# Reading a table of numbers ahead of a loop on TensorE, and routing the first half of the tokens in two steps, in a ViT layer with a two-of-eight mixture of experts

## The chip, the cores and the metric

The kernel runs on one core of one Trainium2 chip. The number that counts is the device time of one execution in microseconds (us). The kernel before took 144.37 us as the median of three runs (144.24 to 144.65). The profiled execution took 144.59 us, of which the trace spans 142.8.

TensorE (PE) multiplies, VectorE (DVE), ScalarE (ACT) and GpSimd (POOL) work on tiles in SBUF and PSUM, SyncE (SP) issues transfers. Each engine takes its instructions in the order in which the program writes them, and waits on semaphores where the program says so.

## The reference

Sixteen images of 128 by 128 are cut in 64 patches each. One layer is computed, all of it in float32:

```python
g       = noisy_linear(patches, W1);  inner = noisy_linear(patches, W2)
h       = (g * tanh(softplus(g)) * inner) @ W3.T + b3 + position     # 16 x 64 x 128
h       = concat(cls_tok, h)                                          # one class row per image
n       = layernorm(h)
q, k, v = split(n @ w_qkv)                                            # 8 heads of 16
dots    = where(causal, q @ k.T * scale, 0)
t       = dots - cum_mean(dots);  s = cum_mean(t * t)                 # no softmax: a running norm
attn    = where(causal, t * rsqrt(s + eps) * norm_g + norm_b, 0)
h       = h + (attn @ v) @ w_out + b_out
x       = layernorm(h)
logits  = x @ router_w;  top 2 of 8 experts, gates = softmax of the two
y_e     = layernorm(x + relu(x @ w1[e] + b1[e]) @ w2[e] + b2[e]) * gamma[e] + beta[e]
out     = h + sum over the two experts of gate * y_e
```

The class row is the same for all images, so it is computed once and the layer works on 1025 rows.

## The kernel before

**Tiles.** The 1024 patch rows are 8 tiles of 128, with the class row as a ninth tile (number 4) between the two halves. Attention goes by four groups of four images (two tiles each). For each group PE makes scores into PSUM banks 0 to 3, DVE masks them into `D` (`evict`), ACT squares them, PE multiplies with the values (`weigh`) and sums the squares (`sum_squares`), DVE forms means and scales (`head_sums`, `mix`), PE projects (`turn_mixed`, `output`), and DVE adds the residual and normalises (`residual_sums`, `normalise_group`). The part of the sum that comes from the class key is the table `tab`. In the kernel before, PE adds it into the bank of the projection with a product of the identity and `tab` at the end of `sum_values` (line 1257).

**Routing.** The tokens are routed in three parts: the first half with the class row (tiles 0 to 4), then two tiles, then two tiles. For a part, PE turns the normalised rows (`turn_norm2`), ACT copies them out of PSUM (`copy_norm2`), PE multiplies with the router (`route`), DVE picks the top two (`choose`) and forms 0/1 tables (`rank_tables`), PE counts ranks with them (`rank_bases`, `rank`), and DVE makes row numbers of them (`places`). The gates of the first part are computed on POOL (lines 471 to 479), the others on DVE (`gates`) from an exponential on ACT. POOL then scatters each row twice to DRAM with indirect DMAs, 16 in all (`dispatch`, line 464): eight for the first half, four for each later part.

**The loop over slots.** The rows stand in DRAM sorted by expert, and 23 tiles of 128 rows (slots) are run through an expert each. The first five slots have a fixed expert; for the other 18 DVE computes the expert and the tile number (`slot_tiles`; its last step is line 1002, semaphore `slots_done`). Each engine that needs these numbers reads them from SBUF into registers, four with one load (`four_values`, line 323 in the profile). SP needs them for the transfers, ACT for the first seven, PE for the address of the second weight. PE reads four at a time inside the loop, at slots 5, 9, 13, 17 and 21. Per slot PE turns the rows (1430), multiplies with the first weight (1438) and one slot later with the second (1457); ACT applies relu (684), DVE normalises (1054 to 1076), and POOL adds the bias (498) and sends the rows back to DRAM (503). The last four slots are not sent: PE adds them with products of 0/1 matrices (1482).

**Filler.** `keep_warm(n, bank)` is n products of zeros that nobody reads (line 1150). Ten of them (`REWARM`) stand ahead of the loop, behind a wait for `token_cols_set`, which POOL sets after its last scatter (line 490). PE's order around the loop is this:

```python
pe.wait_ge(token_cols_set, 1)
keep_warm(REWARM, 7)
pe.wait_ge(slots_done, 2)
pe.wait_ge(w2_loaded, 16)
pe.wait_ge(base_done, 3)
turn_slots(0)
```

All orders are written out by hand; there is no scheduler.

Of the kernel before, what the change touches and what calls it, by code (L numbers as in the profile page):

```python
# [10 lines left out]
ALU = mybir.AluOpType  # L11
# [30 lines left out]
PART_AT, PART_T = [0, CLS + 1, CLS + 1 + CT // 2], [CT, CT // 2, CT // 2]  # L42
PATCH_TILE = [0, CT, CT + CT // 2]
# [35 lines left out]
def vit_tower(nc, patches, noise, body, b1, w1b1, w2, gb2, out):  # L79
    ctx = ExitStack()  # L80
    with ctx:  # L81
# [49 lines left out]
        minus_one = sb("minus_one", [P, NT])  # L131
# [78 lines left out]
        WARM, KEEP_WARM, REWARM = 16, [11, 12, 2, 2, 5, 3, 1, 2, 1, 3, 2], 10  # L210
        TABLES = 9 + PARTS
        X2_BANK, LG_BANK, RANK_BANK, COUNT_BANK, GATE_BANK = [6, 0, 4], [7, 1, 5], [2, 3, 6], 0, 7
# [70 lines left out]
        first_gates = sem("first_gates")  # L283
# [59 lines left out]
        def _(sp):  # L343
# [29 lines left out]
            sp.wait_ge(first_gates, 4)  # L373
# [27 lines left out]
            for j in range(FIXED, FIRST_ROWS):  # L401
                load_pack(j)
# [20 lines left out]
        def _(pool):  # L423
            nc.gpsimd.memset(e_base[:, :], math.e).then_inc(pow_const, 1)
            nc.gpsimd.memset(minus_one[:, :], -1.0).then_inc(pow_const, 1)
# [27 lines left out]
            pool.wait_ge(pow_const, 2)  # L453


            def dispatch(t, c):
                pool.wait_ge(row_at_done, c + 1)
                if c == 0:
                    pool.wait_ge(first_gates, 4)
# [16 lines left out]
            pool.wait_ge(first_gates, 2)  # L476
            nc.gpsimd.tensor_tensor(x2k[:, a:b, 0, P + 1], den[:, a:b], minus_one[:, a:b], ALU.pow).then_inc(first_gates, 1)
            pool.wait_ge(first_gates, 3)
# [38 lines left out]
        def _(act):  # L517
# [92 lines left out]
            def copy_norm2(c):  # L610

                a = PATCH_TILE[c] * P
                act.wait_ge(x2T_ps, c + 2)
                nc.scalar.copy(x2T[:, a:a + PART_T[c] * P], ps[:, X2_BANK[c], 0:PART_T[c] * P]).then_inc(x2T_done, 1)
# [32 lines left out]
            nc.scalar.copy(x2T_cls[:, :], ps[:, LG_BANK[0], BANK - 1:BANK]).then_inc(x2T_cls_done, 1)  # L647
            square(2)
            copy_norm2(0)
# [7 lines left out]
            copy_norm2(1)  # L657
# [50 lines left out]
        def _(dve):  # L708
# [207 lines left out]
            def residual_sums(g):  # L916
                at = GROUP_AT[g]
                dve.wait_ge(proj_ps, g + 2)
                nc.vector.tensor_tensor(acc[:, at:at + GT, :], ps[:, 6 + g % 2, GT * P:2 * GT * P].rearrange("p (t d) -> p t d", d=P),
# [7 lines left out]
            def choose(c):  # L927
                a, b = ROUTED[c]
                n = b - a
                dve.wait_ge(logits_ps, c + 1)  # L930
                dve.wait_ge(tables_set, TABLES)
                for t in range(a, b):
                    nc.vector.max(top[:, t, :], ps[:, LG_BANK[c], (t - a) * SW:(t - a) * SW + EXPERTS]).then_inc(topped, 1)
                dve.wait_ge(topped, b)
                nc.vector.tensor_tensor(dlt[:, a:b], top[:, a:b, 1], top[:, a:b, 0], ALU.subtract).then_inc(dlt_done, 1)  # L935
                for t in range(a, b):
                    nc.vector.max_index(top_at[:, t, :], top[:, t, :], ps[:, LG_BANK[c], (t - a) * SW:(t - a) * SW + EXPERTS]).then_inc(top_index, 1)
# [88 lines left out]
            choose(1)  # L1026
            normalise_group(3)
# [3 lines left out]
            choose(2)  # L1031
# [4 lines left out]
            dve.wait_ge(first_gates, 4)  # L1036
# [85 lines left out]
        def _(pe):  # L1122
# [60 lines left out]
            def cls_column():  # L1183
# [3 lines left out]
                nc.tensor.transpose(ps[:, LG_BANK[0], BANK - 1:BANK], x2[0:1, CLS, :], ident[0:1, 0:1]).then_inc(x2T_ps, 1)  # L1187
# [48 lines left out]
            def sum_values(g):  # L1236
# [11 lines left out]
                if g == 2:  # L1248
                    pe.wait_ge(x2T_done, 1)
                if g == 3:  # L1250
                    pe.wait_ge(top_index, ROUTED[0][1])
                for i in range(GI):
                    n = GI * g + i
                    mm(ps[PATCHES * (i % 2):PATCHES * (i % 2 + 1), 6 + g % 2, i // 2 * P:(i // 2 + 1) * P], after[:, :],
                       vb[:, n, :, 0:2 * HD], start=True, stop=True)
                pe.wait_ge(tab_set, 1)
                mm(ps[:, 6 + g % 2, GT * P:2 * GT * P], ident, tab[:, :].unsqueeze(1).to_broadcast([P, GT, P]),
                   start=True, stop=False).then_inc(vsum_ps, 1)

            def weigh(g, lo=0, hi=GI):  # L1260
# [5 lines left out]
                if g >= 2:  # L1266
                    pe.wait_ge(oT_done, g - 1)
                for i in range(lo, hi):
# [25 lines left out]
            def output(g):  # L1294

                pe.wait_ge(oT_done, g + 1)
                for t in range(GT):
                    last = mm(ps[:, 6 + g % 2, (GT + t) * P:(GT + t + 1) * P], oT[:, (g * GT + t) * P:(g * GT + t + 1) * P], bd("wout"),
                              start=False, stop=(t == GT - 1))
                last.then_inc(proj_ps, 1)  # L1300

            def turn_norm2(c):

                if c == 0:
                    pe.wait_ge(acc_done, 2)
                else:
                    pe.wait_ge(D_done, GROUPS)
                for i in range(PART_T[c]):
                    t = PART_AT[c] + i
                    pe.wait_ge(x2_done, PATCH_TILE[c] + i + 2)  # L1310
                    last = nc.tensor.transpose(ps[:, X2_BANK[c], i * P:(i + 1) * P], x2[:, t, :], ident)
# [258 lines left out]
```

## Time and profile before

| | |
|---|---|
| median of 3 runs | 144.37 us (144.24 to 144.65) |
| profiled execution | 144.59 us, span 142.8 us |
| PE busy | 130.9 us, 92% of the span |
| DVE / ACT / POOL busy | 104.4 / 72.9 / 57.3 us |
| start of the loop over slots (first product, line 1438) | 84.83 us |
| end of the loop (first product of line 1482) | 129.73 us |

The page's first table counts an engine as busy while an instruction runs. PE is busy 92% of the span, but some of that is filler and some of it runs at half clock. So the chain of waits and the timelines say more than the shares.

### The profile page before, as it was taken

How to read it: one execution, taken by the hardware profiler on the slowest of the kernel's cores; microseconds unless marked ns; L12 is line 12 of the kernel's file. 1: busy time of each engine (PE TensorE's matmuls, PEld its weight loads, DVE VectorE, ACT ScalarE, POOL GpSimd, SP SyncE). 2: the span in 40 equal slices, each digit the busy share in tenths (PEclk: the TensorE clock that was granted, in tenths of full speed). 3: DMA queues.
4: the chain of work that ended last, by engine and by line, in shares of the span. 5: the costliest groups of instructions: out<-in, count | busy, mean ns of one | idle time of the engine just before them, and what ended most of it. 6: DMA issues, size and time to landing. Idle time of an engine off the chain costs nothing. (4 is left out here: it accounts for less than half of the span.)

```text
span 142.8 us, 3886 instructions
## 1 busy us (share of the span) xinstructions
PE 130.9 (92%) x1210; PEld 114.2 (80%) x1210; DVE 104.4 (73%) x417; ACT 72.9 (51%) x214; POOL 57.3 (40%) x96
## 2 busy tenths in 40 slices
PE   7999899999999999889993899999999999999960
PEld 7944898788759898668930879999999999999950
DVE  1479999979988667778664029887878789988580
ACT  5534315834476531139900006887878977896000
POOL 8900000000000046775778131377677767680010
PEclk9999999999999999999555569999999999999999
DMA  4999399999993019611115477598999751015405
GB/s 117 263 457 418 156 387 414 404 339 274 278 270 113 5 17 333 255 50 56 45 56 101 179 166 221 133 317 277 243 334 311 239 163 41 21 33 167 175 0 149
DMA packets 16423, 28.47 MB, mean 199 GB/s; under 512 B 1793, under 2 KB 9878, under 8 KB 16276
## 3 DMA queue, kind: packets, MB, share of 16 engines
q1 hardware_dynamic: 13700, 25.43, 55.3%
q0 software_dynamic: 1152, 2.07, 4.3%
q10 hardware_dynamic: 1552, 0.73, 2.2%
q8 instruction: 10, 0.16, 0.5%
q14 instruction: 9, 0.07, 0.1%
HBM read 19.55 MB, written 12.09 MB: 222 GB/s over the span
## 5 line engine op out<-in xcount | busy, mean ns | idle before, releaser
L1457 PE MATMUL ps<-w_all,hid 128*128 (+1 forms) x184 | 24.7, 278 | 0.3 <-issue 0.2
L1457 PEld LDWEIGHTS ps<-w_all,hid 128*128 128x128 f32 x184 | 22.4, 192 | 1.0 <-issue 0.8
L503 POOL DMA_INDIRECT back<-kTm,xg x16 | 15.9, 997 | 12.2 <-ACT kTm L693 6.1
L684 ACT ACTIVATE hid<-ps,D 128x128 f32<-128x128 f32 x48 | 13.5, 362 | 13.7 <-PE ps L1438 13.7
L1150 PE MATMUL ps<-zeros 128*128 128x128 f32 x112 | 17.8, 312 | 2.9 <-POOL SQ L490 2.9
L1150 PEld LDWEIGHTS ps<-zeros 128*128 128x128 f32 x112 | 16.1, 222 | 3.9 <-POOL SQ L490 3.4
L471 POOL TENSOR_TENSOR ex<-e_base,dlt 128x5 f32<-128x5 f32 x1 | 1.2, 1207 | 44.8 <-DVE dlt L935 44.8
L464 POOL DMA_INDIRECT rows<-x2k,row_at x16 | 16.1, 1007 | 6.9 <-issue 5.0
L1054 DVE COPY xgT<-ps 128x128 f32<-128x128 f32 x23 | 6.7, 290 | 10.1 <-PE ps L1430 8.4
L1438 PE MATMUL ps<-xgT,D 128*128 128x128 f32 x96 | 12.8, 276 | 0.0
L684 ACT ACTIVATE hid<-ps,last_parts 128x128 f32<-128x128 f32 x44 | 12.4, 364 | 0.0
L1438 PEld LDWEIGHTS ps<-xgT,D 128*128 128x128 f32 x96 | 11.7, 192 | 0.1
L1438 PE MATMUL ps<-xgT,last_parts 128*128 128x128 f32 x88 | 11.6, 275 | 0.0
L689 ACT ACTIVATE ysd<-ymv,moe_eps 128x1 f32<-128x1 f32 x23 | 6.8, 294 | 8.4 <-DVE ymv L1063 8.4
L1438 PEld LDWEIGHTS ps<-xgT,last_parts 128*128 128x128 f32 x88 | 10.7, 192 | 0.0
L498 POOL TENSOR_TENSOR xgb<-xg,D 128x128 f32<-128x128 f32 x12 | 6.1, 509 | 5.4 <-issue 4.8
L1061 DVE BATCH_NORM_STATS2 yst<-y 128x6 f32<-128x128 f32 x23 | 6.8, 294 | 0.8
L1131 PE MATMUL ps<-xT_oT,w_noisy 128*128 128x512 f32 x16 | 7.2, 603 | 0.0
L1138 PE MATMUL ps<-zeros 128*128 128x128 f32 x32 | 6.2, 383 | 1.1 <-DVE ln_eps L713 1.1
L1138 PEld LDWEIGHTS ps<-zeros 128*128 128x128 f32 x32 | 6.0, 295 | 1.1 <-DVE ln_eps L713 1.1
L1430 PE MATMUL ps<-body_sb,xg 128*128 128x128 f32 x23 | 6.5, 283 | 0.3 <-DMA xg<-rows 0.2
L693 ACT ACTIVATE kTm<-u,yg 128x128 f32<-128x128 f32 x16 | 6.6, 412 | 0.0
(236 smaller groups left out, 278.4 us busy)
## 6 DMA issues: line engine op xcount, KB each, us to landing
rows<-blank SPq DMA_DIRECT2D x8, 589.5 KB, 6.7
D<-pack SPq DMA_DIRECT2D x12, 386.0 KB, 5.2
last_parts<-pack SPq DMA_DIRECT2D x11, 386.0 KB, 4.8
pack<-w1b SPq DMA_DIRECT2D x1, 2064.0 KB, 15.6
w_all<-w SPq DMA_DIRECT2D x1, 2048.0 KB, 12.2
back<-zeros SPq DMA_DIRECT2D x1, 1152.0 KB, 9.0
xg<-rows SPq DMA_DIRECT2D x16, 65.5 KB, 3.0
xT_oT<-patches SPq DMA_DIRECT2D x2, 512.0 KB, 5.9
```

Source lines behind the costliest of these rows:

```text
L464: nc.gpsimd.indirect_dma_start(rows, bass.IndirectOffsetOnAxis(ap=row_at[:, k, t:t + 1], axis=0), x2k[:, t, k, :], None, bounds_check=EXPE ...
L503: nc.gpsimd.indirect_dma_start(back, bass.IndirectOffsetOnAxis(ap=xg[j][:, P:P + 1].bitcast(U32), axis=0), z[j], None, bounds_check=P * K ...
L684: nc.scalar.activation(hid[j % 2][:, f, :], ps[:, 2 + 2 * (j % 2) + f // 2, f % 2 * P:(f % 2 + 1) * P], ACT.Relu, bias=packed[j % NW][:, H ...
L689: nc.scalar.activation(ysd[j % 2][:, :], ymv[j % 2][:, 1:2], ACT.Sqrt, bias=moe_eps[:, 0:1]).then_inc(y_sd, 1)
L693: nc.scalar.activation(z[j], u[j % 2][:, :], ACT.Copy, scale=yg[j % 2][:, 0:1]).then_inc(z_done, 1)
L1054: nc.vector.tensor_copy(xgT[j % 2][:, :], ps[:, j % 2, 0:P]).then_inc(xgT_done, 1)
L1061: nc.vector.bn_stats(yst[j % 2][:, :], y[j % 2][:, :]).then_inc(y_stats, 1)
L1131: last = mm(ps[:, IN_BANK[c][k], :], w_noisy[:, 2 * k + half, :], xT[:, c, half, :], start=(half == 0), stop=(half == HALVES - 1))
L1138: mm(ps[:, 6, 0:P], zeros[:, :], zeros[:, :], start=True, stop=True)
L1150: mm(ps[:, bank, 0:P], zeros[:, :], zeros[:, :], start=True, stop=True)
L1438: last = mm(ps[:, 2 + 2 * (j % 2) + f // 2, f % 2 * P:(f % 2 + 1) * P], packed[j % NW][:, f * P:(f + 1) * P], xgT[j % 2][:, :], start=True ...
L1457: last = mm(ps[:, 6 + j % 2, 0:P], hid[j % 2][:, f, :], w2_all[:, bass.ds(expert_j, 1), f, :].rearrange("p a n -> p (a n)"), start=(f == 0 ...
```

## The change

The change has these parts.

- **PE's numbers.** PE waits for `slots_done` and reads all 18 expert numbers ahead of the filler and the loop, with five loads in a row. Inside the loop it reads none.
- **SP's order.** SP issues the packs of slots 5 and 6 after the rows of the last four slots, not before.
- **The class key's table.** POOL adds `tab` to `h` for each half (two instructions of 128x512). PE's product with the identity goes, and `residual_sums` waits for the new semaphore `h_tab`.
- **The first half's logits.** The first half is turned and routed group by group: group 0 and the class row ahead of `scores(3)`, group 1 between the two halves of `weigh(2)`. `choose` is called once for tiles 0 and 1 and once for tiles 2 to 4. `sum_values(2)` moves ahead of `scores(3)`, `sum_values(3)` to the place that it leaves. The five fillers ahead of `scores(3)` are gone; two more stand behind `output(2)`. Banks of the logits are other ones, and `output(2)` waits until they have been read.
- **First gates.** The reciprocal goes from POOL (a power of -1) to DVE.
- **The later parts.** DVE normalises the last group after the row numbers of the second part, not ahead of its tables. PE turns the last two tiles after `rank(1)`. ACT computes the second part's exponential ahead of the copy `twice(1)`.

```diff
-        WARM, KEEP_WARM, REWARM = 16, [11, 12, 2, 2, 5, 3, 1, 2, 1, 3, 2], 10
+        WARM, KEEP_WARM, REWARM = 16, [11, 12, 2, 2, 0, 5, 1, 2, 1, 3, 2], 10
...
+            pool.wait_ge(tab_set, 1)
+            for c in range(CHUNKS):
+                pool.wait_ge(xn_done, LN_TILES[c + 1][1] if c else 1 + CT)
+                some = h[:, CHUNK_AT[c]:CHUNK_AT[c] + CT, :]
+                nc.gpsimd.tensor_tensor(some, some, tab[:, :].unsqueeze(1).to_broadcast([P, CT, P]), ALU.add).then_inc(h_tab, 1)
...
-            nc.gpsimd.tensor_tensor(x2k[:, a:b, 0, P + 1], den[:, a:b], minus_one[:, a:b], ALU.pow).then_inc(first_gates, 1)
...
-            for j in range(FIXED, FIRST_ROWS):
-                load_pack(j)
+            expert_at(0)
             tile_at(FIRST_ROWS - FIXED)
             for j in range(SENT, SLOTS):
                 tile_at(j - FIXED)
             for j in range(SENT, SLOTS):
                 load_rows(sp, j, tile_at(j - FIXED))
+            for j in range(FIXED, FIRST_ROWS):
+                load_pack(j)
... ACT
-            twice(1)
             nc.scalar.activation(table_scrap[:, 3:4], zeros[:, 0:1], ACT.Exp)
             exp_gates(1)
-            copy_norm2(2)
+            twice(1)
+            copy_norm2(3)
... DVE
             normalise_group(1)
+            choose(0, GT, 1)
             evict(3)
-            choose(0)
+            choose(GT, CLS + 1, 2, 0)
             rank_tables(0)
             head_sums(2)
+            dve.wait_ge(first_gates, 2)
+            nc.vector.reciprocal(x2k[:, 0:CLS + 1, 0, P + 1], den[:, 0:CLS + 1]).then_inc(first_recip, 1)
             places(0)
...
-            choose(1)
-            normalise_group(3)
+            choose(*ROUTED[1], 3, 1)
             rank_tables(1)
             gates(1)
             places(1)
-            choose(2)
+            normalise_group(3)
+            choose(*ROUTED[2], 4, 2)
... PE, sum_values
-                pe.wait_ge(tab_set, 1)
-                mm(ps[:, 6 + g % 2, GT * P:2 * GT * P], ident, tab[:, :].unsqueeze(1).to_broadcast([P, GT, P]),
-                   start=True, stop=False).then_inc(vsum_ps, 1)
+                last.then_inc(vsum_ps, 1)
... PE
             cls_column()
-            keep_warm(KEEP_WARM[4], 6)
+            turn_norm2(0)
+            sum_values(2)
+            route(0)
             scores(3)
-            turn_norm2(0)
+            turn_norm2(1)
             weigh(2, 0, GI // 2)
-            route(0)
+            route(1)
             weigh(2, GI // 2, GI)
             sum_squares(2)
             rank_bases(0)
             rank(0)
-            sum_values(2)
+            sum_values(3)
             weigh(3)
...
-            w2_experts = {}
+            pe.wait_ge(slots_done, 2)
+            w2_experts = list(range(FIXED))
+            for s in range(0, FREE, 4):
+                w2_experts += list(four_values(mybir.EngineType.PE, expert_of, s, EXPERTS - 1))
...
             pe.wait_ge(token_cols_set, 1)
             keep_warm(REWARM, 7)
-            pe.wait_ge(slots_done, 2)
             pe.wait_ge(w2_loaded, 16)
```

How the orders stand is shown at three places. The first is PE ahead of the loop and in it. In a row of order, L is the line, and ISA is a register instruction. Before, from the product with the gates (1422, 1424), with the reading of slots 5 to 8 at the end:

```order
L1422 MATMUL ps<-beta_sel,gateT 128x512 x2
L1424 MATMUL ps<-beta_sel,gateT 1x128
L1150 MATMUL ps<-zeros 128x128 x10
L1430 MATMUL ps<-body_sb,xg 128x128 x2
...
L1438 MATMUL ps<-xgT,D 128x128 x4
L323 TENSOR_LOAD expert_of
L323 ISA x8
L1457 ISA
L1457 MATMUL ps<-w_all,hid 128x128
```

The same place in the changed kernel, where the pair of a load and its eight register instructions stands four times, and then once with four:

```order
L1441 MATMUL ps<-beta_sel,gateT 128x512 x2
L1443 MATMUL ps<-beta_sel,gateT 1x128
L321 TENSOR_LOAD expert_of
L321 ISA x8
...
L321 ISA x4
L1162 MATMUL ps<-zeros 128x128 x10
L1449 MATMUL ps<-body_sb,xg 128x128 x2
...
L1457 MATMUL ps<-xgT,D 128x128 x4
L1473 ISA
L1473 MATMUL ps<-w_all,hid 128x128
```

Five loads and 36 register instructions have moved from the loop to a place behind the wait for `slots_done` and ahead of the ten fillers.

The second place is PE between `scores(2)` and `weigh(3)`. Before (1187 the class column, 1311 turns, 1321 to 1324 the router, 1254 and 1257 `sum_values`):

```order
L1187 MATMUL ps<-body_sb,x2k 128x1
L1150 MATMUL ps<-zeros 128x128 x5
L1232 MATMUL ps<-qT,kTm 128x64 x16
L1311 MATMUL ps<-body_sb,x2k 128x128 x4
L1272 MATMUL ps<-vb,D 64x34 x8
L1321 MATMUL ps<-body_sb,last_parts 128x28 x4
L1323 MATMUL ps<-body_sb,zeros 128x28
L1324 MATMUL ps<-body_sb,x2T_cls 1x28
...
L1254 MATMUL ps<-vb,after 64x128 x4
L1257 MATMUL ps<-tab,body_sb 128x256
L1272 MATMUL ps<-vb,D 64x34 x16
```

In the changed kernel (1325 turns, 1337 to 1342 the router, 1264 `sum_values`, 1244 the scores):

```order
L1199 MATMUL ps<-body_sb,x2k 128x1
L1325 MATMUL ps<-body_sb,x2k 128x128 x2
L1264 MATMUL ps<-vb,after 64x128 x4
L1337 MATMUL ps<-body_sb,last_parts 128x28 x2
L1341 MATMUL ps<-body_sb,zeros 128x28
L1342 MATMUL ps<-body_sb,x2T_cls 1x28
L1244 MATMUL ps<-qT,kTm 128x64 x16
L1325 MATMUL ps<-body_sb,x2k 128x128 x2
L1282 MATMUL ps<-vb,D 64x34 x8
L1337 MATMUL ps<-body_sb,last_parts 128x28 x2
...
L1264 MATMUL ps<-vb,after 64x128 x4
```

Half of the turns, half of the router's products and the class row now stand ahead of the scores, and the product with `tab` is gone.

The third place is DVE from the choice of the second part. Before (933 to 937 `choose`, 766 and 769 `normalise_group(3)`, 943 to 950 the tables, 957 to 961 the gates, 967 and 972 the row numbers):

```order
L937 MAX_INDEX top_at<-top,ps 128x8 x2
L766 RECIPROCAL rstd<-ln_dev 128x2
L769 TENSOR_SCALAR x2k<-acc,mv,rstd 128x128 x2
L943 TENSOR_TENSOR hot<-iota,top_at 128x2x16
...
L967 TENSOR_TENSOR hot_place<-hot,ps 128x2x16
L972 TENSOR_REDUCE row_at<-hot_place 128x2x2
L933 MAX top<-ps 128x8 x2
```

In the changed kernel:

```order
L946 MAX_INDEX top_at<-top,ps 128x8 x2
L952 TENSOR_TENSOR hot<-iota,top_at 128x2x16
...
L976 TENSOR_TENSOR hot_place<-hot,ps 128x2x16
L981 TENSOR_REDUCE row_at<-hot_place 128x2x2
L769 RECIPROCAL rstd<-ln_dev 128x2
L772 TENSOR_SCALAR x2k<-acc,mv,rstd 128x128 x2
L940 MAX top<-ps 128x8 x2
```

The normalising of the last group has moved behind the row numbers of the second part.

## Rows read from the trace of the kernel before

**Rows 1.** The page, span in 40 slices: PE's granted clock, in tenths.

```profile
PEclk9999999999999999999555569999999999999999
```

**Rows 2.** Chain that ended last, 77 to 96 us: start, duration, what.

```profile
77.05 4.59 DMA rows<-x2k,row_at
...
87.89 0.11 PE ps L1430
...
95.47 0.11 PE ps L1430
```

**Rows 3.** PE's timeline, 72 to 127 us: start, duration, instructions (f32 products show as two).

```profile
72.03 3.78 PE L1422 MATMUL ps<-beta_sel,gateT 72*128 72x512 f32 x4 [0.35 <-ACT gateT L671]
...
79.20 4.64 PE L1150 MATMUL ps<-zeros 128*128 128x128 f32 x20 [2.88 <-POOL SQ L490]
84.00 0.90 PE L1430 MATMUL ps<-body_sb,xg 128*128 128x128 f32 x2 [0.16 <-DMA xg<-rows]
84.83 1.16 PE L1438 MATMUL ps<-xgT,D 128*128 128x128 f32 x8
...
85.94 1.06 PE L1438 MATMUL ps<-xgT,last_parts 128*128 128x128 f32 x8
...
95.42 1.06 PE L1438 MATMUL ps<-xgT,D 128*128 128x128 f32 x8
...
126.87 1.06 PE L1438 MATMUL ps<-xgT,D 128*128 128x128 f32 x8
```

**Rows 4.** DVE's timeline, end of the slot numbers.

```profile
73.62 0.18 DVE L1002 TENSOR_SCALAR tile_of<-tile_f 128x18 int32<-128x18 f32 x1
```

**Rows 5.** Line 323 on ACT, whole span: ns min/median/max, first and last start.

```profile
L323 ACTq TENSOR_LOAD <-tile_of x1: 508/508/508, 73.8 to 73.8; - x1
```

**Rows 6.** Line 323, window 94 to 97 us.

```profile
L323 PEldq SEQ_ASSERT  x4: 18/18/28, 95.4 to 96.4; - x4
L323 PEldq TENSOR_LOAD <-expert_of x1: 556/556/556, 94.5 to 94.5; - x1
```

**Rows 7.** Line 323, window 102 to 105 us.

```profile
L323 PEldq FUSED_REGOPS  x4: 146/148/151, 103.1 to 103.9; - x4
...
L323 PEldq TENSOR_LOAD <-expert_of x1: 340/340/340, 102.7 to 102.7; - x1
```

**Rows 8.** PE's timeline, 45 to 58 us.

```profile
45.63 1.38 PE L1150 MATMUL ps<-zeros 128*128 128x128 f32 x10
47.14 1.12 PE L1232 MATMUL ps<-qT,kTm 32*128 32x64 f32 x32
48.19 0.66 PE L1311 MATMUL ps<-body_sb,x2k 128*128 128x128 f32 x4
...
49.62 1.07 PE L1321 MATMUL ps<-body_sb,last_parts 128*128 128x28 f32 x8
50.54 0.39 PE L1323 MATMUL ps<-body_sb,zeros 128*128 128x28 f32 x2
...
54.29 0.70 PE L1257 MATMUL ps<-tab,body_sb 128*128 128x256 f32 x2
```

**Rows 9.** DVE's timeline, 65 to 68 us.

```profile
65.28 0.60 DVE L769 TENSOR_SCALAR x2k<-acc,mv,rstd 128x128 f32<-128x128 f32 x2
...
67.12 0.19 DVE L972 TENSOR_REDUCE row_at<-hot_place 128x4 uint32<-128x32 f32 x1
```

**Rows 10.** ACT's timeline, the load of the exponential's table.

```profile
64.67 1.28 ACT L660 ACT_TABLE_LOAD   x1
```

**Rows 11.** POOL's timeline, 68 to 85 us and 123 us.

```profile
68.11 0.97 POOL L464 DMA_INDIRECT rows<-x2k,row_at  x1 [1.57 <-DVE row_at L972]
...
84.00 0.45 POOL L498 TENSOR_TENSOR xgb<-xg,D 128x128 f32<-128x128 f32 x1 [4.85 <-issue]
...
123.25 0.99 POOL L503 DMA_INDIRECT back<-gT,xg  x1 [0.91 <-ACT gT L693]
```

More of the change, by code:

```diff
@@ L646, in _ @@
             act.wait_ge(x2T_ps, 1)
-            nc.scalar.copy(x2T_cls[:, :], ps[:, LG_BANK[0], BANK - 1:BANK]).then_inc(x2T_cls_done, 1)
+            nc.scalar.copy(x2T_cls[:, :], ps[:, CLS_COL_BANK, BANK - 1:BANK]).then_inc(x2T_cls_done, 1)
+            copy_norm2(0)
             square(2)
-            copy_norm2(0)
+            copy_norm2(1)
             square(3)
@@ L1296, in output @@
                 pe.wait_ge(oT_done, g + 1)
+                if g == 2:
+                    pe.wait_ge(top_index, ROUTED[0][1])
                 for t in range(GT):
                     last = mm(ps[:, 6 + g % 2, (GT + t) * P:(GT + t + 1) * P], oT[:, (g * GT + t) * P:(g * GT + t + 1) * P], bd("wout"),
-                              start=False, stop=(t == GT - 1))
+                              start=True, stop=True)
                 last.then_inc(proj_ps, 1)
@@ L1304, in turn_norm2 @@
                 if c == 0:
-                    pe.wait_ge(acc_done, 2)
-                else:
+                    pe.wait_ge(v_done, 2 * GROUPS)
+                if c == 1:
+                    pe.wait_ge(x2T_done, 1)
+                if c == 2:
                     pe.wait_ge(D_done, GROUPS)
[L1308 to L1311, printed above, removed]
+                for i in range(GT):
+                    pe.wait_ge(x2_done, GT * c + i + 2)
+                    at = X2_AT[c] + i * P
+                    last = nc.tensor.transpose(ps[:, X2_BANK[c], at:at + P], x2[:, GROUP_AT[c] + i, :], ident)
                 last.then_inc(x2T_ps, 1)
@@ L1316, in route @@
                 pe.wait_ge(x2T_done, c + 1)
-                pe.wait_ge(x2T_cls_done, 1)
+                if c == 1:
+                    pe.wait_ge(top_index, GT)
+                part = max(c - 1, 0)
                 router_wide = body_sb[:, BODY_AT["router"][0]:BODY_AT["router"][0] + SW]
-                for i in range(PART_T[c]):
-                    at = (PATCH_TILE[c] + i) * P
-                    last = mm(ps[:, LG_BANK[c], i * SW:(i + 1) * SW], x2T[:, at:at + P], router_wide, start=True, stop=True)
+                for i in range(GT):
+                    at = LG_AT[part] + (GROUP_AT[c] - ROUTED[part][0] + i) * SW
+                    last = mm(ps[:, LG_BANK[part], at:at + SW], x2T[:, (c * GT + i) * P:(c * GT + i + 1) * P], router_wide, start=True, stop=True)
                 if c == 0:
-                    mm(ps[:, LG_BANK[c], CLS * SW:(CLS + 1) * SW], zeros[:, :], router_wide, start=True, stop=True)
-                    last = mm(ps[0:1, LG_BANK[c], CLS * SW:(CLS + 1) * SW], x2T_cls[:, :], router_wide, start=True, stop=True)
+                    pe.wait_ge(x2T_cls_done, 1)
+                    at = LG_AT[0] + CLS * SW
+                    mm(ps[:, LG_BANK[0], at:at + SW], zeros[:, :], router_wide, start=True, stop=True)
+                    last = mm(ps[0:1, LG_BANK[0], at:at + SW], x2T_cls[:, :], router_wide, start=True, stop=True)
                 last.then_inc(logits_ps, 1)
@@ L1392, in _ @@
             turn_mixed(2)
-            sum_values(3)
             output(2)
```

73 lines of the change are left out of this document (34 added, 39 removed).

## The prediction

> **What bounds the kernel now.** I read the chain that ended last first. It ends in the loop over slots, where PE's products follow one another without a gap, and it goes back from there over the loading of the first rows and the landing of the last scatter (81.64) to POOL's run of scatters [rows 2]. So two things set the time: when the loop starts, and how long PE takes in it. Then I read PE's timeline ahead of the loop [rows 3]: PE waits for POOL until 79.20, runs ten fillers (20 passes) at half clock until 83.84, and finds the rows of slot 0 at 84.00. The filler ends only 0.16 us before the data: two chains of nearly the same length meet here. The page's slices show the granted clock at half (1.2 GHz) from slice 20 to 23 and in part of slice 24, which ends at 85.7, and at full (2.4 GHz) elsewhere [rows 1]. In the last step I read line 323, the reading of numbers, since the change moves it into just this stretch [rows 5 to 7].
>
> **The scatters' side.** PE is busy without a gap from 47.14 to the end of `sum_squares(3)`, so what leaves this stretch shortens it [rows 8]. Two of four turns: half of the 0.59 from 48.19 to the next instruction, 0.3. Two of four router products: half of 49.62 to 50.54, 0.46. The zero product and the class row: 0.45, by the nearest row (0.39 for the zero product, overlapped, and one shorter). The product with `tab`: 0.63 of its 0.70. Sum 1.8 us. The work that moves ahead of `scores(3)` (0.3 turns, 0.55 `sum_values(2)`, 0.9 router) takes the place of 1.38 us of filler and 0.1 of waiting, so `scores(3)` starts within 0.3 us of 47.14. DVE's first `choose` lies in its wait for the scores. The two additions on POOL stand where POOL does nothing; by its 128x128 addition of 0.45 us [rows 11] each costs between 0.45 and 1.8, I take 1.6, and nobody waits for them, as the residual that needs them is some 9 us away. The reciprocal moved to DVE (0.2) takes a power off POOL and brings the first scatter forward, but POOL waits for the second part's row numbers anyway (1.57 idle ahead of 68.11 [rows 11]).
>
> The second part's row numbers came at 67.31 [rows 9]. They come 1.8 earlier by PE, and 0.7 earlier since the normalising steps behind them (0.60 and its reciprocal). Of the 0.7 a part is lost to the exponential: the table load of 1.28 us on ACT [rows 10] starts only 0.4 earlier by the moved copy, and the gates wait 0.2 to 0.3 for what follows it. Row numbers at 65.1, so 2.2 earlier. The last eight scatters, the landing of 4.59 us and the rows of slot 0 follow: slot 0's rows would be there at 81.8, and `token_cols_set` at 76.9. Taking the packs of slots 5 and 6 out of this stretch can only shorten the landing; they are wanted ten us later and cost nothing.
>
> **The numbers' side.** What this side needs is `slots_done`, 73.80 [rows 4]. It comes from the last group, and there the gain is given back: the normalising that used to stand at 65.28 now stands behind `places(1)`, which ends at 65.1, so it starts at 65.3 again. Everything behind it (turn, copy, router, ranks, counts, on a PE at half clock) is as before. I take `slots_done` at 73.8, with 0.5 us either way for errors of the sums above.
>
> PE's sequencer can start to read then: the trace shows it reading at 94.5 while products issued before run until 96.48 [rows 3, 6], so the products with the gates (72.03 to 75.8 and one more [rows 3]) do not hold it up. ACT began its own reading at 73.8 [rows 5]. A group of four took PE 1.9 us the first time (94.5 to 96.4), 1.5 us the next (102.7 to 104.2), with 0.27 per number: a register operation of 0.15 and what follows it [rows 5 to 7]. All five in a row: 1.7 for the first with a load of about 0.5, three of 1.45, and 1.0 for the last with two numbers, 7.0 us in all. The bounds are 4.7 (18 numbers at 0.165, the two register instructions of each without what lies between them, and five loads at 0.34) and 8.7 (four groups at the first one's 1.9 and 1.1 for the last); I keep to the pace of rows 7, as nothing but the place is different. So the filler starts at 80.8, not at the 76.9 that POOL would allow. Ten fillers keep the array for 4.4 us at half clock: PE is free at 85.2. Slot 0 starts there, against 84.00, and the products at 86.05 against 84.83: 1.2 later. I add 0.1, since the clock came back shortly before the first product, and would now come back in it. If it returns while the filler runs, the filler is shorter and the delay is 0.6 to 0.8.
>
> The Trainium skill, page "DMA: Bandwidth & Descriptors", section "Latency and other measured facts", gives a floor of about 600 ns for a `tensor_load` and calls unrolling by four the way to spread it. By that figure alone an estimate would be 5 x 0.6 = 3.0 us, numbers at 76.8, and no delay of the filler at all. The rows show a shorter load (0.34 to 0.56) but as much again and more in the register operations behind it, which the page does not count.
>
> **In the loop.** A slot takes (95.47 - 87.89) / 4 = 1.895 us where no numbers are read [rows 2]. From slot 1's product (85.94) to slot 22's (126.87, both [rows 3]) there are 21 steps, 39.7 us at that pace (the last has no turn, 0.11), and it took 40.9: 1.2 us are lost at the reads, 0.47 of them at the first, about 0.2 to 0.3 at each of the next three. All of it comes back to PE. Of the end, DVE's last additions wait for the rows sent back, and the send at 123.25 waited for slot 16's result [rows 11], which lies behind the first three reads only. So I count 0.9 to 1.2, and take 0.95. What could swallow it is DVE, whose work per slot adds up to about 1.8 us, close to PE's 1.895; 0.2 of loss there is in the range.
>
> **The sum.** Against the profiled execution: +1.25 at the start, -0.95 in the loop, +0.3 in all, so 144.9 against 144.59. The median of the runs is 0.2 lower, so I forecast 144.6. The gain of 2.2 us on the scatters is hidden behind PE's numbers and filler. Its own range is 144.0 to 145.2. A difference of 0.3% (0.43 us) is about what a measurement of this kernel can tell from none.
>
> **Rivals.**
> - *The filler shrinks.* The numbers take 6 us or less, and the clock returns within the filler, as it would if it came at the time of before (84.6) regardless of PE's start. PE free at 84.6, products 0.6 later or less, loop -1.1: -0.5 to -0.9, 143.6. For it: passes take 0.11 at full clock and 0.22 at half. Against: before, the clock came back only after all of the filler was done. Chance 0.22.
> - *The numbers cost only their loads.* Then the full 2.2 us come through, and 0.95 in the loop: 144.4 - 3.15 = 141.2. For it: between 103.1 and 104.2 half of the time is not spent in a register operation. Against it: even without those gaps the reading ends at 78.5 [rows 7], behind POOL's 76.9. Chance 0.05. The floor per load on the Trainium skill's page on DMA leads to this case.
> - *The clock returns late.* PE now stands idle from 76.3 to 80.8, not to 79.2, at half clock. If the clock comes back one slice of the page (3.57 us) later than 86.2, all products until then run at half pace: 1.8 us more, in all +2.0, 146.4; half a slice gives 145.5. The same mechanism acts earlier too: less work on PE after 58 us may let the clock fall before the last group is routed (it fell near 67.5), which moves `slots_done` by 0.5. It decides from about 1 us of half clock inside the loop on. For it: the stretch has long gaps already; against: the filler is as long as before and ends right at the loop. Chance 0.20.
> - *The change on the first half fails*, that is, PE does not gain the 1.8 us, as DVE's `choose` or POOL's gates hold up `rank(0)`. Then `slots_done` moves as well, by what is missing, up to 1.5 us: 145.2 to 146. Chance 0.05.
>
> **Chances and range.** The forecast has 0.48, of which 0.06 lies above the band of no change and 0.04 below. Faster by over 0.3%: 0.04, 0.18 of the 0.22 of the first rival, and 0.05, 0.27 in all. Slower by over 0.3%: 0.06 + 0.20 + 0.05 = 0.31, to which I move 0.03 from the band for a start of the numbers held up by something that the trace does not show. Within: 0.38 + 0.04 - 0.03 = 0.39. The range that leaves out 2 in 10 is 143.4 to 146.0.
>
> **What the changed profile would show.** PE's reading (five loads, no product between them) from about 73.8 to 80.8; PE's idle time ahead of the filler ended by nothing on POOL, whose last instruction ahead of it (line 490 before) ends near 77; first slot at 85.2 with its rows landed some 3 us before; the last scatter issued near 74.9, not 77.05; all steps of the loop 1.89 us. A loop that starts before 83, or a filler that waits for POOL again, would make the forecast wrong, and so would a clock row with a sixth slice at half.

## The result and the profile after

The changed kernel took 146.03 us (median, 145.87 to 146.42) against 144.48 us for the kernel before on the same chip: a ratio of 1.0113, 95% interval 1.0086 to 1.0139. It is 1.55 us slower, where no change was forecast (144.6) and the range ended at 146.0.

The page's clock row and the landmarks of PE and DVE answer to [rows 1], [rows 3] and [rows 4]. First the granted clock in 40 slices of the changed kernel's span of 144.0 us:

```profile
PEclk9999999999999999997555558999999999999997
```

It has five slices at half clock with a part of one on either side, against four and a part before [rows 1].

PE's timeline of the changed kernel (start, duration, instructions). Line 1441 is the product with the gates, 1162 the filler, 1449 the turn of a slot's rows, 1457 the first product:

```profile
72.47 3.78 PE L1441 MATMUL ps<-beta_sel,gateT 72*128 72x512 f32 x4 [0.35 <-ACT gateT L674]
...
82.17 4.63 PE L1162 MATMUL ps<-zeros 128*128 128x128 f32 x20 [5.40 <-issue]
86.60 0.64 PE L1449 MATMUL ps<-body_sb,xg 128*128 128x128 f32 x2
87.40 1.16 PE L1457 MATMUL ps<-xgT,D 128*128 128x128 f32 x8 [0.17 <-DVE xgT L1066]
...
131.18 2.17 PE L1497 MATMUL ps<-gT,xT_oT 128*128 128x128 f32 x18
```

The filler used to start at 79.20, after 2.88 us of waiting for POOL. It starts at 82.17 now, after 5.40 us of "issue", which is time in which the profile shows no other engine that it waits for. What PE's sequencer (the part of the engine that takes the instructions and reads the registers) does in it stands in line 321, window 73 to 83 us (duration in ns, first and last start), beside the last step of the slot numbers on DVE and two POOL instructions. The first stands behind the last scatter, and the second is the first use of slot 0's rows, so that they have arrived by then:

```profile
L321 PEldq FUSED_REGOPS  x18: 146/146/165, 75.1 to 81.9; - x18
L321 PEldq SEQ_ASSERT  x18: 18/18/24, 75.3 to 82.1; - x18
L321 PEldq TENSOR_LOAD <-expert_of x5: 331/347/590, 74.4 to 81.0; - x5
```

```profile
74.16 0.18 DVE L1011 TENSOR_SCALAR tile_of<-tile_f 128x18 int32<-128x18 f32 x1
```

```profile
76.63 1.14 POOL L492 IOTA SQ<- 128x1152 f32 x1
80.91 0.45 POOL L500 TENSOR_TENSOR xgb<-xg,D 128x128 f32<-128x128 f32 x1 [3.15 <-issue]
```

Three chains stand side by side. Scatters: POOL's last instruction starts at 76.63, not 78.03, and slot 0's rows are there by 80.91, not at 84.00 [rows 3, 11]. That is 3.1 us of gain, but PE touches these rows only at 86.60. Numbers: they are ready for reading at 74.34, not at 73.80, and read by 82.1. Filler: 4.4 us behind that. The first product comes 2.57 us later than before (87.40 against 84.83), and from there to the last stage 43.78 us pass instead of 44.90, 1.12 less. The sum is +1.45 us. The medians differ by 1.55 us, and the two profiled executions (145.87 and 144.59) by 1.28: the last stage and what follows it took 0.17 less in the changed one.

### The profile page after: what moved, and what is told of

It is laid out like the page before. It is cut to its first block and busy times, and to the rows that moved or that the text cites. A ratio compares the mean times of both kernels' runs of the same rounds, so it can differ in the third digit from the quotient of the medians.

```text
span 144.0 us, 3863 instructions
## 1 busy us (share of the span) xinstructions
PE 126.7 (88%) x1196; PEld 112.1 (78%) x1196; DVE 104.3 (72%) x418; ACT 73.0 (51%) x215; POOL 58.1 (40%) x96
## 5 line engine op out<-in xcount | busy, mean ns | idle before, releaser
L1162 PE MATMUL ps<-zeros 128*128 128x128 f32 x106 | 16.9, 314 | 5.4 <-issue 5.4
L1162 PEld LDWEIGHTS ps<-zeros 128*128 128x128 f32 x106 | 15.3, 224 | 6.4 <-issue 6.4
L470 POOL TENSOR_TENSOR h<-h,tab 128x512 f32<-128x512 f32 x2 | 2.5, 1266 | 28.5 <-DVE tab L909 23.7
L1150 PE MATMUL ps<-zeros 128*128 128x128 f32 x32 | 5.9, 370 | 1.1 <-DVE ln_eps L716 1.1
L1071 DVE TENSOR_TENSOR y<-ps,xgb 128x128 f32<-128x128 f32 x23 | 6.5, 282 | 0.1
L1150 PEld LDWEIGHTS ps<-zeros 128*128 128x128 f32 x32 | 5.7, 282 | 1.1 <-DVE ln_eps L716 1.1
```

The source lines that it names most:

```text
L1150: mm(ps[:, 6, 0:P], zeros[:, :], zeros[:, :], start=True, stop=True)
L1162: mm(ps[:, bank, 0:P], zeros[:, :], zeros[:, :], start=True, stop=True)
```

## The experiments

Three landmarks serve in every run: the end of the slot numbers on DVE (line 1002 or 1011), the first product of the loop, and the first product of the last stage. The two stretches between them can be compared even where the time of a whole run can't. Runs e1 to e4 and f1 to f4 fell on two chips on which the kernel before took 150 to 156 us (medians 152.39 and 153.83), and whose traces hold a long wait between 56 and 67 us of the span (last section). For those the stretches and the ratio to the kernel before on the same chip are used; the intervals are wide, and no trace of the kernel before was kept from these chips. Runs g1 to g4 and h1 to h4 fell on two other chips, on which the medians of the kernel before were 144.56 and 144.41 us.

Two theories run through the expectations. Theory 1: the reading of the 18 numbers and then the filler, one behind the other, set the start of the loop. Theory 2: this reading costs nothing, and another part of the change costs the time.

| run | numbers to first product | first product to last stage | ratio to before (95%) |
|---|---|---|---|
| before (profile) | 11.03 | 44.90 | |
| changed (profile) | 13.06 | 43.78 | 1.0113 (1.0086 to 1.0139) |
| e1 reads in the loop | 8.72 | 44.82 | too few runs |
| f1 the same | 8.72 | 44.93 | too few runs |
| h1 the same | 8.71 | 44.82 | 0.9894 (0.9839 to 0.9948) |
| e2 before, reads ahead | 13.20 | 44.22 | 1.0121 (1.0008 to 1.0234) |
| f2 the same | 12.59 | 43.82 | 1.0113 (1.0061 to 1.0164) |
| e3 reads between fillers | 8.74 | 43.77 | 0.9932 (0.9868 to 0.9996) |
| e4 more filler at rank(1) | 12.86 | 43.95 | 1.0188 (1.0076 to 1.0300) |
| g4 the same | 12.72 | 43.80 | 1.0133 (1.0064 to 1.0202) |
| g1 changed, again | 12.61 | 43.78 | 1.0135 (1.0081 to 1.0188) |
| g2 no filler | 8.82 | 46.13 | 0.9938 (0.9904 to 0.9973) |
| g3 filler first | 12.56 | 46.14 | 1.0221 (1.0151 to 1.0290) |
| f3 reads in loop, packs back | 9.14 | 45.12 | 0.9816 (0.9732 to 0.9901) |
| h2 the same | 8.90 | 45.02 | 0.9924 (0.9897 to 0.9951) |
| f4 four groups, more filler | 7.34 | 45.20 | 0.9681 (0.9583 to 0.9779) |
| h4 the same | 7.38 | 43.80 | 0.9732 (0.9690 to 0.9773) |

**The reads undone (e1, f1, h1).** The changed kernel with `four_values` back in `second_product` (shortened; the function again reads four numbers when it meets a slot that has none yet):

```diff
-            pe.wait_ge(slots_done, 2)
-            w2_experts = list(range(FIXED))
-            for s in range(0, FREE, 4):
-                w2_experts += list(four_values(mybir.EngineType.PE, expert_of, s, EXPERTS - 1))
+            w2_experts = {}            # four numbers are read at slots 5, 9, 13, 17, 21
...
             keep_warm(REWARM, 7)
+            pe.wait_ge(slots_done, 2)
```

> The changed kernel, but PE reads the expert numbers four at a time inside the loop again and waits for slots_done behind the filler; all else as changed. Theory 1 (reading 18 numbers and then the filler, in series, set the start of the loop): the filler starts with POOL's last instruction near 77.9 and ends near 82.3, the first product of the loop starts near 83.0 instead of 87.4, and the loop loses about 1.1 us at the reads again: 146.0 - 4.4 + 1.1 = 142.7 us. Theory 2 (the first half's new order or SP's new order costs the time): the time stays at 146 us or above, since the loss in the loop comes on top.

> The same kernel as e1 (the changed kernel with PE's reads inside the loop again), beside others on one chip. From slot numbers (end of the last step of slot_tiles) to the first product of the loop both theories can be read in the trace: theory 1 expects 8.7 us as in e1 against 13.1 in the changed kernel, and 1.1 us more inside the loop, so 3.3 us off the changed kernel and 1.8 off the kernel before. Theory 2 (the first half's order costs) expects it no faster than the kernel before.

> The kernel of e1 and f1 (reads in the loop, all else as changed), once more. On a chip where the kernel before takes 144.5 us, theory 1 expects 142.2 to 142.9 us (8.7 us from the slot numbers near 74.5 to the first product, 1.1 us lost in the loop); the theory that the rest of the change costs time as well expects 144 us or more.

Measured: 143.27 us in h1 against 144.41 (ratio 0.9894). The interval lies below the kernel before and, beside g1's 1.0135, below the changed kernel. On the other chips the medians were 149.84 against 152.39 (e1) and 150.70 against 153.83 (f1), of four runs each. The stretch from numbers to first product is 8.71 us in all three, and the 1.1 us in the loop are back. PE's timeline of h1:

```profile
78.28 4.64 PE L1162 MATMUL ps<-zeros 128*128 128x128 f32 x20 [1.05 <-POOL SQ L492]
82.72 0.60 PE L1449 MATMUL ps<-body_sb,xg 128*128 128x128 f32 x2
83.52 1.16 PE L1457 MATMUL ps<-xgT,D 128*128 128x128 f32 x8 [0.20 <-DVE xgT L1066]
```

The filler waits for POOL again, and slot 0's rows, in use on POOL at 80.60, now wait for the filler: 2.1 us. So theory 1 holds, and the rest of the change is a gain by itself. My figure for h1 (142.2 to 142.9) was 0.4 to 1.1 us too good. Its first product came at 83.52 and not near 83.0, since POOL's last instruction ran at 77.09 and not at 76.63 as in the changed kernel's trace; what the rest is, the traces don't tell.

**The reads alone (e2, f2).** The kernel before with the reverse edit.

> The kernel before, and of the change only PE's reading ahead of the filler and the loop. Theory 1: the numbers are there at 73.8 + 7.7 = 81.5, the filler ends near 85.9, the first product starts near 86.7 instead of 84.83, and the loop gains 1.1: 144.5 + 1.9 - 1.1 = 145.3 us. Theory 2: the reads cost nothing at this place and the loop gains, 143.4 us.

> The same kernel as e2 (the kernel before with the reads ahead of the filler alone). Theory 1: 13.2 us from slot numbers to first product against 11.0 before, 1.1 us back in the loop: 1.0 us slower than the kernel before, ratio 1.007. Theory 2: 0.8% faster than before.

Measured: ratios 1.0121 and 1.0113, both intervals above 1. By the ratios, the edit that moves five reads costs as much on the old order as the whole change does. The two stretches show less of it: against the kernel before, e2's add up to 1.5 us more and f2's to 0.5, of some 1.7 by the ratios. Nothing on record shows where the rest lies. In e2 the clock came back only within the first product (1.61 us long, 1.16 in f2), which accounts for the 0.4 by which its loop took longer than f2's.

**Reads between the fillers (e3).** Two fillers stand ahead of each of the five reads, and PE doesn't wait for POOL any more (shortened):

```diff
-            pe.wait_ge(slots_done, 2)
-            w2_experts = list(range(FIXED))
-            for s in range(0, FREE, 4):
-                w2_experts += list(four_values(...))
+            pe.wait_ge(slots_done, 2)
+            for s in range(0, FREE, 4):
+                keep_warm(2, 7)
+                read_experts(s)
...
-            pe.wait_ge(token_cols_set, 1)
-            keep_warm(REWARM, 7)
```

> The changed kernel, with the ten fillers spread over the five reads (two ahead of each) and without the wait for POOL's last instruction. Theory 1: only the reading (7.7 us from 74.4) is left in series, the rows of slot 0 are there at 80.9, so the first product starts near 83.0: 4.4 us earlier, 141.6 us with a clock that returns as early relative to the loop as before. Rival on the clock: fillers with pauses of over a microsecond between them do not bring the clock back, the first products run at half pace until it returns, and up to 1.8 us of it are lost: 143.4 us. Theory 2: 146 us.

Measured: first product 8.74 us after the numbers, not 13.06, with the loop as short as in the changed kernel (43.77). The clock was at full by the first product (1.16 us for its eight passes), so in this execution the rival on the clock did not occur; it did once in h3, below. The time was a miss: a ratio of 0.9932 is 143.5 us where the kernel before takes 144.5, and not 141.6. The interval allows 142.6 to 144.4, and the runs don't tell where the rest of the gain went.

**More filler behind `rank(1)` (e4, g4).** One line, `keep_warm(4, 2)`, ahead of `turn_norm2(3)`.

> The changed kernel with four more fillers behind rank(1), where PE stood idle for 1.1 us ahead of turning the last two tiles. If the early fall of the clock (near 65 instead of 67.5) came from this idle stretch, the clock stays up as before, slots_done comes 0.5 us earlier than 74.35 and the whole is 0.5 us faster: 145.5 us. If the fall does not hang on this stretch, nothing changes: 146.0 us, or 0.1 to 0.3 more by fillers in the way of the turn.

> The same kernel as e4 (the changed kernel with four more fillers behind rank(1)), beside the changed kernel on the same chip. If the earlier fall of the clock comes from PE's idle stretch there, the clock stays at full through the ranks of the last part, the slot numbers come 0.5 to 1.1 us earlier, and the whole is 0.5 to 1.1 us faster than g1. Rival: the clock falls anyway, no difference.

Inconclusive. The trace of g4 has the clock at full through 66 to 68 us and the numbers at 73.50, 1.2 us earlier than g1's 74.71, but the medians are the same (145.95 and 146.01), with g4's runs from 144.9 to 146.9. In the same window the granted clock was 0.50 in g1 and 0.72 in the changed kernel's first trace, so two executions of one kernel already differ. One profiled execution with more filler and a late fall of the clock does not show that the filler caused it.

**No filler (g2), filler first (g3), and the changed kernel beside them (g1).** g2 sets `REWARM` to 0. g3 moves the wait for `token_cols_set` and the ten fillers ahead of the wait for `slots_done` and the reads.

> The changed kernel itself, beside the next three on one chip. Both theories: 1.1% slower than the kernel before; from slot numbers to first product 13.1 us.

> The changed kernel with no filler ahead of the loop (REWARM 0). Theory 1 (reads and filler in series): the first product comes 4.5 us earlier, 8.6 us after the slot numbers, but at half clock. If the clock comes back as long after PE's start as it did with the filler (5.2 us), the first slots lose 2.6 us: 1.9 us less than the changed kernel in all. Rival (the filler is what brings the loop up to pace and is worth its time): as slow as the changed kernel or slower.

> The changed kernel with the filler ahead of the wait for slots_done and of the reads, behind POOL's last instruction. If PE's sequencer runs ahead of the array, the reads begin about 1 us after the filler starts (near 79 instead of 74.4) and end near 86.7: the first product 13 us after the slot numbers, as in the changed kernel, within 0.7 us. The array then idles 4 us between filler and loop, so the clock can fall back or stay down and the first slots lose up to 2.6 us: 0 to 2.6 us slower than the changed kernel. If the sequencer waited for the array, the first product comes 3.5 us later still.

g2 took 143.89 us, 2.1 less than g1, 1.9 expected. The first product comes 3.8 us sooner after the numbers and the loop takes 2.35 longer, as it starts at half clock. That is 1.4 us; of the rest, the numbers came 0.2 earlier in g2's trace and what follows the start of the last stage was 0.7 shorter. PE's timeline of g2, then of g3:

```profile
82.53 0.66 PE L1449 MATMUL ps<-body_sb,xg 128*128 128x128 f32 x2 [5.55 <-issue]
83.36 2.08 PE L1457 MATMUL ps<-xgT,D 128*128 128x128 f32 x8 [0.17 <-DVE xgT L1066]
```

```profile
78.34 4.31 PE L1162 MATMUL ps<-zeros 128*128 128x128 f32 x20 [1.05 <-POOL SQ L492]
86.59 0.66 PE L1449 MATMUL ps<-body_sb,xg 128*128 128x128 f32 x2 [3.94 <-issue]
87.42 2.08 PE L1457 MATMUL ps<-xgT,D 128*128 128x128 f32 x8 [0.17 <-DVE xgT L1066]
```

The first product takes 2.08 us at half clock against 1.16 with the clock back. In g3 the array (the part that multiplies) ran the filler from 78.34 to 82.65 while the sequencer was already reading: its loads start at 79.0. Had it waited for the array, the reads would have ended past 90, and they end at 86.4. The loop starts as long after the numbers as g1's and takes 2.4 us more: 147.85 us, 1.8 slower than g1. The filler had brought the clock back (granted 0.96 from 82 to 84 us and 0.90 from 84 to 86), and after the 3.94 us without a product it was at 0.50 from 86 to 92. So here the filler was worth its place only right ahead of the loop, and in series with the reads it costs more (4.4) than the clock it saves (2.4).

**The first half alone (f3, h2).** h1's kernel, with SP's packs of slots 5 and 6 ahead of the rows again. What is left of the change is the first half's order, POOL's table and the exponential.

> The changed kernel with PE's reads in the loop, and SP issuing the packs of slots 5 and 6 ahead of the rows again. If these two transfers (0.77 MB) had lengthened the landing of the last scatter, the rows of slot 0 come up to 2 us later than in f1; the filler ends 4.5 us after POOL's last instruction, which hides about half of that: 0 to 1 us slower than f1. If they did not matter, the same time as f1.

> The kernel of f3 (the changed kernel without its two parts on numbers and packs: the first half's order, POOL's table, the exponential), on the same chip as h1. f3 had the rows of slot 0 4 us after POOL's last instruction at the scatter, as the kernel before, and started the loop 0.5 us later than f1. Expected: 0.4 to 0.8 us slower than h1, 1.2 to 1.8 us faster than the kernel before.

h2 took 143.42 us (0.9924), h1 143.27 (0.9894): no difference that these intervals can tell, though both beat the kernel before. The traces differ where they should. POOL's timeline of h1 and of h2, the instruction behind the last scatter and the first use of slot 0's rows:

```profile
77.09 1.14 POOL L492 IOTA SQ<- 128x1152 f32 x1
80.60 0.45 POOL L500 TENSOR_TENSOR xgb<-xg,D 128x128 f32<-128x128 f32 x1 [2.37 <-issue]
```

```profile
77.62 1.14 POOL L491 IOTA SQ<- 128x1152 f32 x1
83.54 0.45 POOL L499 TENSOR_TENSOR xgb<-xg,D 128x128 f32<-128x128 f32 x1 [4.78 <-issue]
```

With the packs in between it takes 5.9 us to the rows, without them 3.5. The pair f1 and f3 shows the same, 3.4 and 6.1. The filler hides nearly all of the 2.4: from POOL's instruction to the first product it takes 6.6 us in h2 and 6.4 in h1. The packs are not all there is to it, though. The profiled execution of h3, below, has no packs in this stretch and took 5.9 us as well.

**Four groups ahead among the fillers (h3), and with more filler at `rank(1)` (f4, h4).** e3's edit with four groups read ahead and fillers of 2, 3, 3 and 2 ahead of them, the fifth group in the loop; f4 and h4 add g4's line.

> The changed kernel with four groups of numbers read ahead among the ten fillers, the fifth in the loop, no wait for POOL's last instruction; nothing at rank(1). Theory 1: the first product 7.4 to 7.7 us after the slot numbers against 12.9, so 5.2 us off the changed kernel's 146.0: 140.8 us. If the clock is still at half when the loop starts, up to 1.8 us less gain.

> The changed kernel with the first four groups of numbers read ahead and the ten fillers spread over these four reads, the last group read in the loop (at slot 21, where the kernel before lost nothing), no wait for POOL's last instruction, and four more fillers behind rank(1). Theory 1: 6.3 us of reading after the slot numbers; the rows of slot 0 are there about 6.5 us after them, the first product 7.4 us after them against 13.1, and the loop as short as in the changed kernel: 5.2 to 5.7 us off the changed kernel, 140.5 us where that takes 146.0. If the spread fillers leave the clock at half in the first slots, up to 1.8 us of it is lost. Theory 2: 146 us.

> h3 with four more fillers behind rank(1), the kernel of f4. If the idle stretch there makes the clock fall early, 0.5 to 1.1 us faster than h3, near 140.0; if the clock's fall does not hang on it (e4 and g4 left that open: the trace had the slot numbers 1.1 us earlier, the median of the runs did not move), equal to h3.

h3 took 141.10 us (ratio 0.9761, 0.9722 to 0.9801), h4 140.66 us (0.9732, 0.9690 to 0.9773). Both beat both kernels; against each other they are not told apart. f4's ratio on its own chip, 0.9681, says the same (its loop lost 1.4 us in a single step at slot 2, where PE waited 1.15 us for DVE, which h4 did not). PE's timeline of h4:

```profile
77.89 4.39 PE L1162 MATMUL ps<-zeros 128*128 128x128 f32 x20
82.23 0.41 PE L1450 MATMUL ps<-body_sb,xg 128*128 128x128 f32 x2
82.91 1.16 PE L1458 MATMUL ps<-xgT,D 128*128 128x128 f32 x8 [0.28 <-DVE xgT L1066]
...
126.71 2.17 PE L1505 MATMUL ps<-gT,xT_oT 128*128 128x128 f32 x18
```

and line 321 of the same kernel on PE's sequencer:

```profile
L321 PEldq FUSED_REGOPS  x16: 146/146/165, 76.2 to 81.8; - x16
L321 PEldq TENSOR_LOAD <-expert_of x4: 333/336/558, 75.6 to 80.6; - x4
```

The fillers (77.89 to 82.3) and the reads (75.6 to 82.0) lie side by side instead of one behind the other, slot 0's rows (81.41 on POOL) wait less than a microsecond, and the loop loses nothing (43.80).

It does not always go so well. The execution of h3 that was profiled took 144.00 us, 2.9 above its median, and so has no row in the table. PE's timeline of it:

```profile
83.20 0.44 PE L1449 MATMUL ps<-body_sb,xg 128*128 128x128 f32 x2 [1.92 <-DMA xg<-rows]
83.89 2.07 PE L1457 MATMUL ps<-xgT,D 128*128 128x128 f32 x8 [0.24 <-DVE xgT L1066]
```

PE was ready and waited 1.92 us for slot 0's rows, and the first product ran at half clock: both the rows and the clock can come late, and then most of the gain is gone.

## Why the prediction was wrong

**The mechanism was the forecast one.** PE's reads start when the slot numbers are there, the filler follows them, the rows of slot 0 have been lying there for microseconds, and the gain on the scatters is hidden. e1, f1 and h1 take the reads away and e2 and f2 add them alone; both agree in direction. "Reading at 94.5 while products issued before run" holds at the new place (74.4, under the products from 72.47), and g3 shows it again.

**The step that failed is the size of the start's delay.** The prediction put the first product at 86.05 + 0.1 and counted "+1.25 at the start" (its own figures give 1.3). It came at 87.40, +2.57. That is 1.25 later than 86.15: +0.5 by the slot numbers, +0.8 by the reading, -0.1 by the rest.

- *The reading: 7.0 us forecast, 7.7 measured* (74.4 to 82.1; from the numbers at 74.34 to the filler at 82.17 it is 7.8). I worked it out from the cheapest group's pace [rows 7] with one dear load in front. The five starts in the changed kernel lie 1.8, 1.7, 1.5 and 1.6 us apart, and the last group takes 1.1. The five groups of the kernel before add up to the same: 1.9, 1.5, 1.5, 1.6 and 1.1 are 7.6. The trace held all five: the last three loads start at 110.5, 118.3 and 126.1, and their groups end at 112.0, 119.9 and 127.2. Every group was counted a little too cheap: 1.7, three times 1.45 and 1.0, against 1.8, 1.7, 1.5, 1.6 and 1.1. The floor of about 600 ns per load, which the prediction cited from the Trainium skill, page "DMA: Bandwidth & Descriptors", section "Latency and other measured facts", did not hold for these loads: they took 0.33 to 0.59 us. They add up to some 2.0 of the 7.7 us; the rest is the register operations (18 times 0.16, so 2.9) and the gaps between them.
- *The slot numbers: 73.8 forecast, 74.34 measured.* The claim "everything behind it is as before" failed. DVE's normalising started at 65.26 (65.3 forecast) and the turn at 65.66, but the router's products took 0.93 us and not 0.63, for the clock fell sooner. The stretch at 66 to 68 us in the kernel before and in the changed one (busy time of PE, PEld, DVE, ACT and POOL, then PEclk, DMA share and GB/s):

```profile
66.00:68.00 2.00, 2.00 (x16) 1.83 (x15) 1.73 (x14) 1.96 (x8) 0.54 (x1) 0.88 0.11 36
```

```profile
66.00:68.00 2.00, 1.54 (x8) 1.35 (x8) 0.30 (x3) 1.72 (x6) 1.70 (x2) 0.72 0.12 38
```

  A mean of 0.88 against 0.72 between levels of 1.0 and 0.5 puts the fall near 67.5 and 66.9. The prediction had this as part of a rival ("moves `slots_done` by 0.5"), with the right size. That PE's idle stretch behind `rank(1)` is the cause is argued only: e4 and g4 did not settle it. One more thing lies here that nobody tried. PE reads `expert_of` alone, which DVE had written at 73.73 (line 1006, the first of the two signals of `slots_done`), but waits for both signals, so for `tile_of` at 74.34. A wait for the first one alone might start the reading 0.6 us earlier.
- *The rest, -0.1*: the filler took 4.4 us, as forecast, and PE was free at 86.60. The first product came 0.80 behind the start of the turn, which ran at half clock (0.64 us for two), where 0.85 and the 0.1 for the clock had been counted.

**What was right.** The first half: `scores(3)` at 47.29 ("within 0.3 us of 47.14"), `weigh(3)` at 53.27 against 54.92 (1.65 of 1.8 us), the second part's row numbers at 64.96 plus 0.19 (65.1 forecast). The last scatter came at 75.67 and not at 74.9: the last part's row numbers came at 71.05 and POOL waited 1.09 us for them, which I had not counted. It did not set the time, as PE came later still. Slot 0's rows came at 80.9, and not at 81.8. The prediction had said that moving the packs could only shorten the landing; the pair h1 and h2 shows it by 2.4 us, with h3's execution as the exception. The loop gave 1.12 us (0.95 forecast, bounds 0.9 to 1.2); DVE did not take it back.

**The rivals.** "The numbers cost only their loads" is refuted by the row of line 321. "The filler shrinks" needed numbers in 6 us or less, and they took 7.7. Its other half occurred in part: from the filler's start to the turn it took 4.43 us in the changed kernel's first trace, and 4.19 in g1, 4.25 in g4 and 3.94 in f2, whose turns ran at full clock (0.38 us for two). It shortens the start by up to 0.5 us and never by enough. "The clock returns late" did not occur in the changed kernel: the first product took 1.16 us as before. It did where the filler was missing or stood early, in g2 and g3, for 2.3 and 2.4 us, and in part in e2 and in h3's execution. "The change on the first half fails" is refuted by `weigh(3)` at 53.27 and by h2, which beats the kernel before.

## What to carry to other kernels

Work that is taken out of a loop goes somewhere, and "ahead of the loop" is a place with a chain of its own: before moving it, find which chain ends last there and whether the moved work stands in series with it. Filler for the clock and a sequencer's register work can lie over one another, as g3 and h4 show. With the reads first and the filler behind them they cost 7.7 and 4.4 us in series; interleaved, all five reads with the ten fillers took 8.1 us from the numbers to the first turn (e3), four reads 6.7 (h4). And add up all rows of the thing that is moved instead of multiplying the cheapest one.

## What the runs showed of the hardware

- Reading 18 numbers from SBUF into PE's registers took 7.7 us in the changed kernel and in g1, and 7.9 with fillers in between (e3): five loads of 0.33 to 0.59 us, and about 0.27 us per number, of which 0.164 are the two register instructions.
- In the loop the same reads cost only 1.1 us in all (44.90 against 43.78): the sequencer runs ahead of the array, as the load at 94.5 under products that run until 96.48 shows, and most of the reading lies under products that are already issued. The last group, read at slot 21, cost nothing that shows: PE's step there is 1.90 us long, as where nothing is read.
- Two transfers of 386 KB each, issued in h2 0.5 and 1.1 us after the last scatter began, came with rows of slot 0 that arrived 2.4 us later than in h1 (f3 against f1: 2.7). The five traces with these packs have 4.5 to 6.1 us from POOL's instruction to the rows, twelve of the thirteen without them 3.3 to 4.3, and the last, h3's, 5.9.
- On the chips of e1 to e4 and f1 to f4 PE, DVE and ACT stood still together, while POOL went on: for 2.6 to 2.7 us from 56 us of the span in e1, e3, e4 and f1, for 4.2 in f3 and f4, and for some 1.7 us later, between 63 and 67 us, in e2 and f2. In f1 it is DVE's step at line 845 that comes late, by a wait of 3.5 us that the profile puts down to "remote", and ACT and PE wait behind it. This is f1 (busy time of PE, PEld, DVE, ACT, POOL, then PEclk, DMA share, GB/s), and then the changed kernel's trace for the same stretch, in which they work:

```profile
56.00:58.00 2.00, 0.00 (x0) 0.00 (x0) 0.00 (x0) 0.00 (x0) 1.70 (x2) 1.00 0.97 360
```

```profile
56.00:58.00 2.00, 0.94 (x9) 0.89 (x9) 1.40 (x8) 0.66 (x2) 1.70 (x2) 1.00 0.95 353
```

  The transfers are much the same in both (360 and 353 GB/s), so they alone are not the cause; the runs do not tell it.
